# First layer norm of a two-layer pair kernel: statistics by batch-norm statistics instructions, and another order around them

## What is computed

```python
x = _layernorm(pair_repr, ln1_w, ln1_b)                  # over the 32 features, eps 1e-5
left = jax.nn.sigmoid(x @ left1) * (x @ left2)
right = jax.nn.sigmoid(x @ right1) * (x @ right2)
p = jnp.einsum('nsre,nkre->nske', left, right)           # the triangle product
p = _layernorm(p, ln2_w, ln2_b)
g = jax.nn.sigmoid(jnp.einsum('nsrz,zy->nsry', x, gate))
q = jnp.einsum('nrse,ez->nsrz', p, out_w) * g
return residual + q
```

## Time and profile before

| | us |
|---|---|
| median of 3 runs | 122.13 (121.76 to 123.0) |
| the profiled execution | 122.19 |
| its span in the profile | 120.4 |
| DVE busy | 88.2 (73%) |
| PE busy | 94.3 (78%) |
| ACT busy | 73.6 (61%) |
| POOL busy | 69.6 (58%) |
| first data of x used | 6.8 |
| triangle product starts | 44.8 |

### The profile page before, as it was taken

How to read it: one execution, slowest core, us unless ns; L and a number is a source line. 1 busy time by engine, 2 the same in 40 slices (tenths; PEclk the granted TensorE clock), 3 DMA queues, 4 the chain that set the end, 5 groups by cost and what they waited for, 6 DMA issues and landing times.

```text
span 120.4 us, 1797 instructions
## 1 busy us (share of the span) xinstructions
PE 94.3 (78%) x566; PEld 72.0 (60%) x566; DVE 88.2 (73%) x221; ACT 73.6 (61%) x129; POOL 69.6 (58%) x82
## 2 busy tenths in 40 slices
PE   1954799279779969999584999999999999696000
PEld 1943345167557759965231669888798889596000
DVE  1069999399999890776999635677498989799920
ACT  2245462886997537996138964555997798861100
POOL 5046688706099200884650597957835787995800
PEclk9997555958999999999998599999999999999755
DMA  2799990000000000000000000000000005429796
GB/s 43 140 138 153 147 142 8 0 0 0 5 0 0 0 3 5 0 3 0 0 0 0 0 0 5 0 0 3 0 0 5 0 0 87 75 34 144 109 145 103
DMA packets 33484, 4.51 MB, mean 37 GB/s; under 512 B 33348, under 2 KB 33476, under 8 KB 33476
## 3 DMA queue, kind: packets, MB, share of 16 engines
q1 hardware_dynamic: 32160, 4.06, 26.1%
q10 hardware_dynamic: 1316, 0.35, 1.5%
HBM read 2.31 MB, written 2.10 MB: 37 GB/s over the span
## 4 chain that ended last, share of the span: by engine, by line
PE 38%; DVE 35%; ACT 7%; issue 6%; DMA 5%; POOL 3%; SPq 0%; DVEq 0%; POOLq 0%
DVE lr L614 6%; PE bank L965 6%; PE bank L1008 6%; PE bank L875 5%; DMA x_tok<-in_x 5%; PE bank L1017 4%; DVE sums L585 4%; PE bank L979 3%; POOL acc_q L348 3%; PE bank L982 3%; PE bank L980 3%; DVE sums L570 3%; PE bank L938 3%; DVE lr L794 3%; DVE st L593 2%
## 5 line engine op out<-in xcount | busy, mean ns | idle before, releaser
L875 PE MATMUL bank<-lr_blk,xnT 64*128 64x256 f32 x128 | 21.2, 470 | 5.6 <-DVE lr L614 4.0
L875 PEld LDWEIGHTS bank<-lr_blk,xnT 64*128 64x128 f32 x128 | 14.4, 228 | 9.9 <-ACT xnT L426 5.2
L364 POOL TENSOR_TENSOR x_low<-x1T,x_high 128x512 fp32r<-128x512 f32 x8 | 11.0, 1380 | 12.1 <-ACT x_high L497 12.1
L614 DVE TENSOR_TENSOR lr<-bank,sig_lr 128x512 f32<-128x512 f32 x16 | 15.8, 1041 | 2.6 <-ACT sig_lr L436 2.3
L415 ACT ACTIVATE std<-st,eps 128x16 f32<-128x16 f32 (+4 forms) x14 | 4.4, 317 | 13.0 <-DVE st L600 5.9
L280 POOL TENSOR_TENSOR xc<-x_tok,sums 128x512 f32<-128x512 f32 (+2 forms) x7 | 8.0, 1144 | 7.4 <-DVE sums L578 7.4
L356 POOL TENSOR_TENSOR t_tok<-p_sb,rstd 128x512 f32<-128x512 f32 x7 | 10.4, 1491 | 2.8 <-DVE rstd L751 2.8
L436 ACT ACTIVATE sig_lr<-bank 128x512 f32<-128x512 f32 x16 | 9.4, 598 | 4.0 <-PE bank L875 3.9
L380 POOL TENSOR_TENSOR sq<-lr,row_rep 128x512 f32<-128x512 f32 x7 | 9.8, 1401 | 2.0 <-DVE lr L797 2.0
L965 PE MATMUL bank<-tT,out_blk 128*128 128x512 f32 x16 | 8.9, 638 | 2.2 <-DVE x1T L768 2.2
L372 POOL TENSOR_TENSOR oT<-o_a,rsum 128x512 f32<-128x512 f32 x8 | 8.7, 1090 | 2.5 <-issue 1.9
(11 more groups left out here) (119 smaller groups left out, 236.1 us busy)
## 6 DMA issues: line engine op xcount, KB each, us to landing
x_tok<-in_x SPq DMA_DIRECT2D x14, 128.0 KB, 4.3
out<-sq SPq DMA_DIRECT2D x7, 256.0 KB, 3.3
x_tok<-in_x SPq DMA_DIRECT2D x4, 64.0 KB, 4.6
w_rep<-in_weights ACTq DMA_DIRECT2D x1, 180.5 KB
out<-sq ACTq DMA_DIRECT2D x1, 128.0 KB, 4.5
out<-sq SPq DMA_DIRECT2D x1, 128.0 KB, 4.9
row_rep<-in_rows ACTq DMA_DIRECT2D x1, 32.0 KB, 5.1
```

The costliest lines, as they stand in the source:

```text
L364: nc.gpsimd.tensor_tensor(x1_low[:, c % 2], x1T[:, c % 3], x1_high[:, c % 2], ALU.subtract).then_inc(x1_low_ready, 1)
L614: nc.vector.tensor_tensor(lr[:, :, s].rearrange("p f s -> p s f"), src[:, :, 2 * CH:4 * CH], sig_lr[:, j % 3].rearrange("p (s f) -> p s f" ...
L875: last = nc.tensor.matmul(dst, xnT[half, c, k * P:(k + 1) * P], lr_blk[half].rearrange("p g m c -> p g (m c)"), start=True, stop=True, ski ...
```

## The change

The feature sums, the squares, their sums and the two small steps to the variance are replaced by one kind of DVE instruction, `bn_stats`. Given 64 elements a partition it returns six numbers: count, mean and count times variance of the elements at even places, and the same for those at odd places. Two tokens 2k and 2k+1 are read interleaved (feature 0 of the one, feature 0 of the other, feature 1 of the one, ...), so that the even places are one token and the odd places the other. 64 such instructions cover all tokens. The root reads count times variance (it scales by 1/32 itself), and the centring reads the mean, now with a step of three elements. Further:

- the block of 32 tokens in `SUMS1` becomes two of 16;
- the second transfer of the first block is issued from the ACT queue, ahead of the weights;
- ACT loses all eight squares; its roots, affine steps and sigmoids are reordered (the last three roots stand together behind the fifth sigmoid), and PE's transposes and projections follow that order;
- on DVE the first three multiplications move ahead of the statistics of the later blocks;
- GpSimd normalises block by block at first, and the preparation of the first output projection moves to the end of its list; the two matmuls and the two DVE instructions that use it move behind the last projection and the last multiplication, the matmuls from bank 7 to bank 1.

```diff
-SUMS1 = [(0, 8), (8, 16), (16, 32), (32, 48), (48, 64), (64, 96), (96, 112), (112, 128)]
+SUMS1 = [(0, 8), (8, 16)] + [(16 * n, 16 * n + 16) for n in range(1, 8)]
...
+            lo, hi = SUMS1[0]
+            act.dma_start(place(x_tok[:], lo, hi)[:, 1], x_tok_dram[:, lo + 1:hi:2, :]).then_inc(x_in[0], 16)
             act.dma_start(w_rep[:], weights.rearrange("(a p) n -> a p n", a=1).to_broadcast([GRP, CH, n_w])
...
-                    values, of = stat(std[:, 0], lo, hi), stat(st[:, 0], lo, hi)
+                    values, of = stat(std[:, 0], lo, hi), place(stats1[:, :, 2:3], lo, hi)
...
+            def statistics1(b):
+
                 lo, hi = SUMS1[b]
                 dve.wait_ge(x_in[b], arrived(b))
+                c, half = lo // SPC * SPC, hi - lo < SPC
+                first = lo % SPC // (SPC // 2) * GRP
+                places = [c + 8 * n + first + k for n in range(2) for k in (0, 2)] if half else range(lo, hi, 2)
+                for k in places:
+                    last = nc.vector.bn_stats(stats1[:, k:k + 2, :].rearrange("p s v -> p (s v)"),
+                                              x_tok[:, k:k + 2, :].rearrange("p s c -> p c s"))
+                last.then_inc(stats1_ready, 1)
```

The new order on ACT:

```diff
+            root1_of(0)
+            root1_of(1)
             act.wait_ge(w_in, 16)
             affine1(0)
             root1_of(2)
             affine1(1)
             root1_of(3)
+            sigmoid_lr(0, 0)
             affine1(2)
+            sigmoid_lr(0, 1)
+            affine1(3)
+            sigmoid_lr(1, 0)
+            sigmoid_lr(1, 1)
+            sigmoid_lr(2, 0)
+            for b in (4, 5, 6):
+                root1_of(b)
+            affine1(4)
+            sigmoid_lr(2, 1)
+            for c in range(3, CHUNKS):
+                if c < CHUNKS - 1:
+                    affine1(c + 2)
                 sigmoid_lr(c, 0)
                 sigmoid_lr(c, 1)
```

On DVE, behind the first block:

```diff
+            statistics1(1)
             inverse1(1)
+            statistics1(2)
             inverse1(2)
+            statistics1(3)
             inverse1(3)
+            statistics1(4)
+            multiply_lr(0, 0)
+            multiply_lr(0, 1)
+            statistics1(5)
+            multiply_lr(1, 0)
+            statistics1(6)
+            statistics1(7)
             inverse1(4)
             inverse1(5)
+            statistics1(8)
+            inverse1(6)
+            multiply_lr(1, 1)
+            for c in range(2, CHUNKS):
+                for h in range(2):
+                    multiply_lr(c, h)
```

On TensorE and GpSimd:

```diff
+            project_lr(0, 0)
+            transpose_xn(1)
+            project_lr(0, 1)
+            transpose_xn(2)
+            transpose_xn(3)
+            project_lr(1, 0)
+            project_lr(1, 1)
+            project_lr(2, 0)
+            transpose_xn(4)
+            project_lr(2, 1)
+            for c in range(3, CHUNKS):
+                if c < CHUNKS - 1:
+                    transpose_xn(c + 2)
                 project_lr(c, 0)
                 project_lr(c, 1)
...
             centre(1)
+            normalise1(1)
+            centre(2)
+            normalise1(2)
+            centre(3)
+            normalise1(3)
+            for b in (4, 5, 6):
                 centre(b)
+            for n in (4, 5, 6):
+                normalise1(n)
+                if n < 6:
+                    centre(n + 3)
             for n in (7, 8):
                 normalise1(n)
+            nc.gpsimd.tensor_scalar(out0_scaled[:], mat("out0"), vec("ln2_w"), None, ALU.mult
+                                    ).then_inc(out0_scaled_ready, 1)
+            block_diagonal(out0_raw_blk[:], mat("out0"))
```

More of the change, by code:

```diff
@@ L230, in stat, with mean_of @@
             return place(row.rearrange("p (s a) -> p s a", a=1), lo, hi)
+        def mean_of(lo, hi):
+            v = place(stats1[:, :, 1:2], lo, hi)
+            return v.to_broadcast([P, v.shape[1], v.shape[2], CH])
         def each_feature(row, lo, hi):
@@ L247, in _ @@
                     last = min(first + SPC, hi)
-                    for n in range(2):
+                    for n in range(2 if b else 1):
                         sp.dma_start(place(x_tok[:], first, last)[:, n], x_tok_dram[:, first + n:last:2, :]
@@ L563, in link @@
                 dve.wait_ge(step, steps[0])
-            def add_x(b):
+            def statistics1(b):
                 lo, hi = SUMS1[b]
                 dve.wait_ge(x_in[b], arrived(b))
[L570 to L593, removed]
-                                        ALU.add).then_inc(diff1, last + 1 - first)
-            def variance1(first, last):
-                lo, hi = SUMS1[first][0], SUMS1[last][1]
-                dve.wait_ge(diff1, last + 1)
-                nc.vector.tensor_scalar(stat(st[:, 0], lo, hi), stat(st[:, 0], lo, hi), 0.0, None,
-                                        ALU.max).then_inc(var1, last + 1 - first)
+                c, half = lo // SPC * SPC, hi - lo < SPC
[5 more added lines that the diff above has]
+                last.then_inc(stats1_ready, 1)
             def inverse1(b):
@@ L622, in _ @@
                                            op1=ALU.add).then_inc(centre_ready, 1)
-            add_x(0)
-            mean(0)
-            add_squares(0)
-            difference(0, 0)
-            variance1(0, 0)
+            statistics1(0)
             lo, hi = SUMS1[0]
-            dve.wait_ge(mean1, 1)
-            nc.vector.tensor_tensor(place(xc[:], lo, hi), place(x_tok[:], lo, hi),
-                                    each_feature(sums1[:, 0], lo, hi), ALU.subtract).then_inc(centre0, 1)
-            add_x(1)
+            dve.wait_ge(stats1_ready, 1)
+            nc.vector.tensor_tensor(place(xc[:], lo, hi), place(x_tok[:], lo, hi), mean_of(lo, hi), ALU.subtract
+                                    ).then_inc(centre0, 1)
             inverse1(0)
-            mean(1)
             dve.wait_ge(centre0, 1)
@@ L867, in project_lr @@
                 for n in range(2):
-                    if j == 1 and n == 1:
-                        transpose_xn(2)
                     k = 2 * n + h
```

120 lines of the change are left out of this document (19 added, 101 removed).

## The result

The changed kernel takes 116.87 us (median of 4 runs, 116.44 to 117.31) beside 122.28 for the kernel before: ratio 0.9554, 95% interval 0.9488 to 0.9620. That is 5.4 us, twice the 2.5 that were forecast. The time lies just inside the range (116.6 to 122.8); the forecast of 119.6 does not hold. The profiled execution took 117.17 us, 1.8 of it around the span. Executions of one kernel spread by 1 to 4 us, and the ratios leave out those over 1.5% above the fastest of their kernel, which the medians keep.

The account below looks back on a forecast made before the run. DVE was taken to bound the front up to the triangle product; 14.7 us removed less 12.2 added gave 2.5 us, as did the walk: 122.1 - 2.5 = 119.6 us, range 116.6 to 122.8.

Parts of the forecast that it names:

- The bound, and where the gain arises: First data to triangle product: DVE bounds it, busy 34.4 of 38.0 us; a shifted start arrives at the end.
- What is removed from DVE: On DVE in the front: reductions 9.5 us, means and negative squares 1.3, variance steps with waits 3.9; 14.7 us.
- What is added: On DVE in the front: 64 bn_stats at 0.19 us start to start, 12.2 us, bounds 0.12 to 0.25 each.
- The walk: Front in the new order: four projections at half clock hide cheaper bn_stats; triangle product at 42.3, 2.5 us earlier.
- rival A: TensorE's lower clock in the front ends sooner, DVE's work becomes the limit: 4.7 us gained, 117.5 us; chance 0.22.
- The first transfer: Second half of first block issued from ACT's queue: gains 0 to 0.5 us at 6.8, taken back by the projections.
- B: bn_stats on DVE at 0.22 to 0.26 us each: 0 to 1.5 us gained, 121.5 us; chance 0.16.
- C: bn_stats on DVE keeps its whole latency; DVE the bound from 0.26 us each; at 0.30, 2.5 us lost, 124.7; chance 0.14.
- Rival D: Lower-clock stretch behind the triangle product lies on busier work or comes twice: 0.8 us gained in sum, 121.4; chance 0.06.

Follow-up runs that it names:

- half doubling: Changed kernel with every second bn_stats issued twice, the first time into a spare tile: 119.46 us (ratio 0.9761), again 119.39 us (0.9746).
- Fillers: Changed kernel with six more matmuls that nothing reads, on TensorE behind the first transpose: 116.91 us (ratio 0.9558), again 116.44 us (0.9483).

## Why the prediction was off

**The bound, and where the gain arises**: right. The front held the time, the rest followed its start (75.6 and 75.2 us), and DVE's work counted most, as the statistics alone in the old order show (4.6 of 5.5 us). Once it had fallen, it was no longer the sole bound: of 8.1 us put back, 4.0 arrived.

**What is removed from DVE, 14.7 us**: right in kind; L593 and L600 are gone with their waits on GpSimd. DVE's busy time in the front fell by 34.4 - 25.8 = 8.6 us; 14.7 - 8.1 = 6.6 is the forecast's account at the measured price, and 0.61 + 0.42 + 0.20 + 0.42 = 1.65 us of work on the first block now lie between 3.4 and 5.4, ahead of the front as I cut it.

**What is added, 64 x 0.19 = 12.2 us**: this is the step that failed. The term was 8.1 us. The bounds of 0.12 to 0.25 held it, near the lower end, and the estimate of 0.127 us stood beside the sum, which did not use it. I priced the jumps of the interleaved read after the strided multiplication, and no such price shows: 0.127 is the 64 elements at a reduction's rate, 0.067, and 0.06. With the price set back to 0.19 by half doubling, the kernel takes 119.5 and 119.4 us against the forecast of 119.6.

**The walk, by which nothing is gained below 0.20**: this failed with it, for by the walk a `bn_stats` of 0.127 would have left the time at 119.6 all the same. From 0.19 to 0.127 the time falls by 1.7 to 2.7 us (119.4 and 119.5 against 116.8 to 117.7), and the ratios do not touch (0.9675 and up against 0.9669 and down). The walk held projections 1 to 4 in one unbroken run of 9.4 us from 12.8 to 22.2 at half clock. In fact projection 1 began at 12.27, the half clock ended at 15.8, and projections 2 to 4 took 2.86 us together and ended at 19.13; after that TensorE waited 3.8 us for GpSimd's first normalised tokens of the second half, which waited for the statistics and roots ahead of them. The chain shows just that: `bn_stats` at 17.78, GpSimd, and TensorE only from 22.95 or so. The seventh multiplication started at 28.92, not at 31.3 to 32.0, and from there to the triangle product it took 11.2 us, against 10.8 before and in the walk. What the walk had right is the beginning at half speed and, to half a microsecond, this last stretch. That 119.6 came out at 0.19 is in part luck, since the clock took another course there too (half up to 16.6, and again from 23.4).

**The clock, rival A**: its picture is seen (half clock to 15.8, triangle product at 40.2, 116.9 us against its 117.5), but it gave the clock 2.9 of its 4.7 us. Fillers that remove the early stretch leave the median where it was. In single profiles it is worth 1.6 us, and the length of the second stretch 1.3. Its second half, DVE's work becoming the limit at a cheap `bn_stats`, is half right: half of the work put back arrives.

**The first transfer, 0 to 0.5 us at 6.8**: off, it was 3.4 us at the first block. The next block and the weights came only at 7.3, so the first projection gained 0.9 us by it (9.82 against 8.92). It is worth 0.8 us in the old order; in the new one it was not measured clearly. **Rivals B and C**: no; at 0.25 the changed kernel is still 0.0117 x 122.8 = 1.4 us faster than the one before (and with fillers even, 0.9960), so C's point of 0.26 was about right or a little low. **Rival D**: a half-clock stretch on the triangle product exists. It cost 1.3 us in the first profile with half the doubling (76.5 us behind the start instead of 75.2), and it is in one of the three profiles of the changed kernel itself, at 39.8 to 43.2; that execution took 118.25 us although its triangle product started no later:

```profile
39.91 6.31 PE L862 MATMUL bank<-lr 128*128 128x128 f32 x40 [0.54 <-DVE lr L590]
PEclk9995579959999859999999999999999999999965
```

What stays open: the parts of the new block sizes, the new order and the preparations' place, of which only the sum was measured, at 0.8 and 1.5 us, neither firmly; why fillers and the split of the weights reach the same starts of the triangle product and differ in their medians; and what sends the clock on one course or the other.

## What to carry to other kernels

Where a new instruction's price is unknown, take the whole range through the sum, and don't let a walk of the other engines flatten it: the walk's limit depended on a clock that moved. Price it by the rate of the plain instructions on the same memory; a slow row that differs in two things (strided, and from PSUM) is no measure of one of them. When one engine's work shrinks, look at what lands: here the transfers and the weights were next, and a version with the weights' transfer split was faster again, by 1.0 to 2.4 us depending on how the executions are counted. Look at the clock before crediting an early start: here the same edit also took away the early stretch at half speed.

## What the runs showed of the hardware

- `bn_stats` over 64 elements read alternately from two rows 128 bytes apart starts every 0.127 us and lasts 0.21, while GpSimd works beside it. The rule of the Trainium skill (SBUF — State Buffer, "Door 1: The DMA port swizzle") that each access which leaves a 16-byte line pays a penalty has no visible effect on this read: a dense reduction's rate and constant give 64 x 1.05 + 50 ns = 0.117 us, the prediction's lower bound. No run read the same elements densely.
- Two 64 KB transfers issued at 0.73 and 0.74 us on two queues ahead of the weights were used at 3.4 us; one issued at 1.75, beside the weights, landed 5.6 us later. Before, one issued at 1.22 took 5.58 us. That the 180 KB of weights hold up what is issued beside them is likely: splitting them brought the second block forward by 0.7 us. No run left them out.
- Keeping TensorE busy up to the first projection kept its clock full to 22.1 us in one profile and to 20.4 in another, just behind and within its next idle time of 3.7 us (to 21.4 and 21.6). Half speed then lasted 3.4 and 6.8 us, the triangle product started at 38.60 and 39.87, and the median did not move.
- The record of the granted clock can miss a stretch. In both profiles of `bn_stats` in the old order it shows 1.00 at the first projection, whose eight records took 2.08 us, the duration at 0.50; at 1.00 they took 1.14.
